# Key stacks of batch 0 sent first, later loads behind unit 0's queries, and a new order of jobs

## The reference, cut to what matters

```python
# layer 0 attention; layer 1 has the same form, with a mask over the context rows
q = (jnp.einsum('bld,ed->ble', x, Wq) + bq).reshape(b, l, h, dh)
kv = (jnp.einsum('bmc,ec->bme', y, Wkv) + bkv).reshape(b, m, h, 2 * dh)
k, v = (kv[..., :dh], kv[..., dh:])
att = jax.nn.softmax(jnp.einsum('blhd,bmhd->blmh', q, k) * scale, axis=2)
out = jnp.einsum('blmh,bmhd->blhd', att, v).reshape(b, l, d)

x = x + _L0_xattn_ref(_layernorm(x, axis=-1), ctx_768, ...)
x = x + _L0_ffn_ref(_layernorm(x, axis=-1), ...)
x = x + _L1_xattn_ref(_layernorm(x, axis=-1), ctx_768, mask_BxS2_bf1, ...)
x = x + _L1_ffn_ref(_layernorm(x, axis=-1), ...)
```

## Time and profile before

| | us |
|---|---|
| median of 3 runs | 402.03 (400.43 to 406.7) |
| the profiled execution | 399.99 |
| its span in the trace | 398.2 |
| TensorE busy | 306.9 (77%) |
| VectorE busy | 261.8 (66%) |
| ScalarE busy | 157.7 (40%) |
| GpSimd busy | 95.6 (24%) |

### The profile page before, as it was taken

How to read it: one execution, slowest core, us unless ns; L and a number is a source line. 1 busy time by engine, 2 the same in 40 slices (tenths; PEclk the granted TensorE clock), 3 DMA queues, 4 the chain that set the end, 5 groups by cost and what they waited for, 6 DMA issues and landing times.

```text
span 398.2 us, 4774 instructions
## 1 busy us (share of the span) xinstructions
PE 306.9 (77%) x1454; PEld 183.6 (46%) x1455; DVE 261.8 (66%) x682; ACT 157.7 (40%) x253; POOL 95.6 (24%) x103
## 2 busy tenths in 40 slices
PE   3476797788888627215667898898998999999995
PEld 1253433435345312013334325253457868888884
DVE  4457545585728168875777426675358699988883
ACT  3010435245463228231224236464663455454542
POOL 3701181010101079311107000101100761421500
PEclk9999959699999757655556569999999999999999
DMA  8962120300000930301311202000000000000000
GB/s 183 197 176 59 45 45 7 81 2 7 2 7 2 226 74 0 106 2 45 87 27 38 49 1 65 23 5 6 3 0 2 2 0 26 2 16 11 2 27 26
DMA packets 11914, 16.77 MB, mean 42 GB/s; under 512 B 3480, under 2 KB 6632, under 8 KB 11881
## 3 DMA queue, kind: packets, MB, share of 16 engines
q1 hardware_dynamic: 10018, 11.75, 12.0%
q0 software_dynamic: 1472, 4.26, 4.6%
q10 hardware_dynamic: 400, 0.45, 0.6%
HBM read 4.74 MB, written 1.05 MB: 15 GB/s over the span
## 4 chain that ended last, share of the span: by engine, by line
PE 59%; DVE 26%; ACT 5%; issue 4%; POOL 3%; DMA 2%; SPq 0%; DVEq 0%; POOLq 0%; ACTq 0%
PE ps_acc L1092 11%; PE ps_tok L938 6%; PE ps_key L947 5%; DVE mx L642 5%; PE ps_acc L1062 4%; PE ps_acc L1064 4%; PE ps_acc L1063 4%; DVE xn L569 3%; DVE stats L559 3%; PE ps_m L980 2%; PE ps_tok L1049 2%; PE ps_tok L1051 2%; PE ps_tok L1050 2%; PE ps_m L957 2%; POOL kst L347 2%
## 5 line engine op out<-in xcount | busy, mean ns | idle before, releaser
L642 DVE TENSOR_REDUCE mx<-ps_tok 128x4 f32<-128x312 f32 x128 | 57.4, 475 | 36.1 <-PE ps_tok L938 35.2
L445 ACT ACTIVATE big<-ps_key 104x512 f32<-104x512 f32 x96 | 55.2, 595 | 55.5 <-PE ps_key L947 54.3
L938 PE MATMUL ps_tok<-kst,qst 97*128 97x312 f32 x128 | 58.1, 479 | 15.8 <-DVE mx L642 15.4
L336 POOL TENSOR_SCALAR veps<-mv 128x4 f32<-128x4 f32 x16 | 3.7, 230 | 228.3 <-DVE mv L562 228.3
L938 PEld LDWEIGHTS ps_tok<-kst,qst 97*128 97x128 f32 x128 | 30.5, 245 | 51.9 <-DVE mx L642 26.9
L947 PE MATMUL ps_key<-qst,kst 105*104 105x512 f32 x96 | 44.9, 480 | 3.9 <-ACT big L445 2.0
L784 DVE TENSOR_TENSOR qst<-big,qst 128x512 fp32r<-128x512 f32 x64 | 44.3, 692 | 2.2
L782 DVE CAST qst<-big 128x512 fp32r<-128x512 f32 x64 | 27.0, 422 | 9.7 <-ACT big L505 9.5
L505 ACT ACTIVATE big<-ps_tok,b 128x512 f32<-128x512 f32 x32 | 21.9, 689 | 25.1 <-PE ps_tok L1051 24.9
L1092 PE MATMUL ps_acc<-big,vbd 104*32 104x512 f32 x192 | 29.9, 699 | 0.7 <-ACT big L445 0.7
L505 ACT ACTIVATE big<-ps_key,b 128x512 f32<-128x512 f32 x32 | 22.0, 691 | 21.3 <-PE ps_key L1051 20.8
(11 more groups left out here) (193 smaller groups left out, 546.8 us busy)
## 6 DMA issues: line engine op xcount, KB each, us to landing
qst<-qhi SPq DMA_DIRECT2D x64, 64.0 KB, 2.0
qst<-qlo SPq DMA_DIRECT2D x32, 64.0 KB, 2.0
w1f<-in_w POOLq DMA_DIRECT2D x2, 1024.0 KB, 7.9
kst<-rbuf POOLq DMA_DIRECT2D x12, 156.0 KB, 6.1
kst<-rbuf SPq DMA_DIRECT2D x12, 156.0 KB, 7.5
x<-in_x SPq DMA_DIRECT2D x4, 256.0 KB, 8.3
out<-xn SPq DMA_DIRECT2D x4, 256.0 KB, 2.0
qst<-mthl SPq DMA_DIRECT2D x32, 16.0 KB
```

What stands on the lines that cost most here:

```text
L445: act.activation(p[:, j, :], key[n % 2][0:PR, :], ACT.Exp, scale=SCALE).then_inc(q["p_ready"], 1)
L642: nc.vector.tensor_reduce(mx[:, u % 2, t, g, 0, :], tok[n % 2][:, 0:KG].rearrange("p (j h) -> p h j", h=HG), AX.X, ALU.max).then_inc(q["to ...
L938: mm(tok[n % 2][:, 0:KG], qst[0:MASKROW + 1, s, g, 128 * t:128 * t + 128], kst[0:MASKROW + 1, b, g, :], start=True, stop=True).then_inc(q[ ...
```

## The change

- The widening is a function of a range of batches. `key_split(0)` widens batch 0 only and raises `k_first`; a new job `kwide`, behind `lnx0` 0 on VectorE, widens batches 1 to 3 and raises `k_split`.
- GpSimd issues twelve transfers for batch 0, computes `rstd` of batch 1, waits for `k_split`, issues twelve for batches 1 to 3, and computes `rstd` of batches 2 and 3. The second twelve have semaphores of their own (`kst_in[2]`), for which `tok` of units 1 to 3 and `key_split(1)` wait.
- SP issues the mask, FFN weights, `bo` and `clip` behind unit 0's twelve query moves and ahead of unit 1's.
- The numbers of the order are new. What they change on the engines: in layer 0 TensorE does `vr0` twice before unit 0's `q`, the first `tok` before unit 1's `xt`, `q` of the next unit behind `tok` 7 instead of `tok` 2 (unit 1 to 3), `key` 0 behind four `tok` of the next unit instead of two, `ot` a `tok` later; VectorE does `on` 0 before `round` 1. In layer 1 TensorE does `xt` of the unit after next before `max` (for `max` 0 and 1), and `key` comes closer together; VectorE does `hround` 3 behind `tok` 5 instead of `tok` 14, and `lnx` 3 behind unit 5's `tok` 7 instead of `tok` 4.

```diff
         AT = (
             dict(
-            xt=[-32.1],
-            q=[-29.6],
-            tok=[-15.5 + 0.75 * c for c in range(NT * G)],
-            max=[-4],
-            pv=[7.1, 8.1, 11.4, 12.1, 15.1, 16.1],
+                xt=[-32.091],
+                q=[-26.662],
+                tok=[-16.267 + 0.753 * c for c in range(NT * G)],
+                max=[-4],
+                pv=[7.1, 8.1, 11.4, 14.206, 15.1, 16.1],
...
             dict(
-            xt=[-32.3],
-            q=[-29.3],
-            max=[-3.9],
-            key=[2 + 0.85 * j for j in range(NC * G)],
+                xt=[-35.965],
+                q=[-29.652],
+                max=[-3.203],
+                key=[1.987 + 0.733 * j for j in range(NC * G)],
...
-        BESIDE = dict(vr0=[-28.6, -25, -12.2, -10.4], lnstat=[-34.5, -26, -12, 4], lnx0=[-34, -23, -8, 8],
-                      nt=[29.8, 46.3, 62.3, 78.3], round=[12, 20, 28], wqt=[46, 48, 51, 53], kt=[55], vr=[56.1, 58, 60.8, 62.1])
+        BESIDE = dict(
+            kwide=[-30.2],
+            vr0=[-27.461, -27.296, -11.925, -9.845],
+            lnstat=[-35.568, -23.099, -13.806, 4.078],
+            lnx0=[-30.348, -21.819, -9.915, 7.66],
+            round=[14.104, 19.969, 30.533],
...
-        FFN = dict(hround=[-42, -41, -15, -5], down=[-40.1, -31.7, -13.1, -3.1], lnx=[-37.6, -25, -9, 4],
-                   gset=[30], x1=[31.1, 48.6], experts=[64.5 + 0.914 * n for n in range(NH)])
+        FFN = dict(
+            hround=[-50.361, -41, -15.005, -11.191],
+            down=[-37.329, -31.874, -12.818, -0.755],
+            lnx=[-35.088, -27.34, -9.108, 5.898],
+            experts=[64.5 + 0.952 * n for n in range(NH)],
...
@@ SP
+            def late_loads():
+                sp.dma_start(cmask[:, :, 0:M], a["mask"].partition_broadcast(128)).then_inc(q["mask_in"], 16)
...
+                        if u == 0:
+                            late_loads()
@@ GpSimd
-            pool.wait_ge(q["k_split"], 1)
-            for g in range(G):
-                for r, half in enumerate((0, 0, 1)):
-                    pool.dma_start(kst[32 * r:32 * r + 32, :, g, :].bitcast(F32),
...
-            for b in range(1, B):
+            pool.wait_ge(q["k_first"], 1)
+            key_stack(0, 1, kst_in[0])
+            rstd_of(1)
+            pool.wait_ge(q["k_split"], 1)
+            key_stack(1, B, kst_in[2])
+            for b in range(2, B):
                 rstd_of(b)
@@ VectorE, key_split
-                for half, src in enumerate((khi, klo)):
-                    for hh_ in range(HG):
-                        ins = nc.vector.tensor_scalar(kbd[:, half, :, hh_], src[:, :].bitcast(F32), kmask[:, hh_:hh_ + 1], None, ALU.mult)
-                ins.then_inc(q["k_split"], 1)
+                if L == 0:
+                    keys_widened(0, 1).then_inc(q["k_first"], 1)
+                else:
+                    keys_widened(0, B).then_inc(q["k_split"], 1)
...
+                    if job == "kwide":
+                        keys_widened(1, B).then_inc(q["k_split"], 1)
@@ TensorE, tok
+                            if L == 0 and b > 0:
+                                pe.wait_ge(kst_in[2][g], 48)
```

More of the change, by code:

```diff
@@ L198, in build @@
         stack_q = [[sem(f"stack_q{i}_{g}") for g in range(G)] for i in range(2)]
-        kst_in = [[sem(f"kst_in{i}_{g}") for g in range(G)] for i in range(2)]
+        kst_in = [[sem(f"kst_in{i}_{g}") for g in range(G)] for i in range(3)]
         stack_m = [[sem(f"stack_m{i}_{g}") for g in range(G)] for i in range(2)]
@@ L235, in build @@
-        BESIDE = dict(vr0=[-28.6, -25, -12.2, -10.4], lnstat=[-34.5, -26, -12, 4], lnx0=[-34, -23, -8, 8],
-                      nt=[29.8, 46.3, 62.3, 78.3], round=[12, 20, 28], wqt=[46, 48, 51, 53], kt=[55], vr=[56.1, 58, 60.8, 62.1])
-        FFN = dict(hround=[-42, -41, -15, -5], down=[-40.1, -31.7, -13.1, -3.1], lnx=[-37.6, -25, -9, 4],
-                   gset=[30], x1=[31.1, 48.6], experts=[64.5 + 0.914 * n for n in range(NH)])
+        AT = (
+            dict(
+                xt=[-32.091],
+                q=[-26.662],
+                tok=[-16.267 + 0.753 * c for c in range(NT * G)],
+                max=[-4],
+                key=[2 + 1 * j for j in range(NC * G)],
+                pv=[7.1, 8.1, 11.4, 14.206, 15.1, 16.1],
+                copy=[16.595],
+                on=[19.082],
+                ot=[21.311],
+                wo=[23.746],
+                ln=[26.718],
+            ),
+            dict(
+                xt=[-35.965],
+                q=[-29.652],
+                tok=[-15.5 + 0.75 * c for c in range(NT * G)],
+                max=[-3.203],
+                key=[1.987 + 0.733 * j for j in range(NC * G)],
+                pv=[6.352, 9.141, 11.1, 11.9, 14.244, 16.391],
+                copy=[17.2],
+                on=[19.768],
+                ot=[22.384],
+                wo=[23.775],
+                ln=[25.942],
+            ),
+        )
@@ L245, in build @@
         AT_YT, AT_Y, AT_LOG, AT_A, AT_B, AT_C = HLAG + 2, HLAG + 3, 12, 13, 15, 5
         FIRST_LOG, FIRST_A, FIRST_B, FIRST_C = 5, 6, 8, 12
-        ACT_LATE = dict(copy=0.4, key=0.2)
-        DVE_LATE = dict(on=0.1)
+        ACT_LATE = dict(copy=0.467, key=0.01)
+        DVE_LATE = dict(on=0.145)
         def order(L, late={}):
@@ L270, in _ @@
             sp.dma_start(kextra[96:97, :], a["krow"]).then_inc(q["mask_in"], 16)
[L271 to L278, removed]
+            def late_loads():
+                sp.dma_start(cmask[:, :, 0:M], a["mask"].partition_broadcast(128)).then_inc(q["mask_in"], 16)
+                for w, src in ((wg0, a["w_gate"]), (wu0, a["w_up"])):
+                    sp.dma_start(w[:, 0:2, :], src[0:256, :].rearrange("(t p) d -> p t d", p=128)).then_inc(q["wffn_in"], 16)
+                    sp.dma_start(w[0:IT[2], 2, :], src[256:I0, :]).then_inc(q["wffn_in"], 16)
+                sp.dma_start(wd0[:, :], a["w_down"]).then_inc(q["wffn_in"], 16)
+                sp.dma_start(bo[:, :], a["bo"].partition_broadcast(128)).then_inc(q["bo_in"], 16)
+                sp.dma_start(clip[:, :], a["clip"].partition_broadcast(128)).then_inc(q["clip_in"], 16)
             def move(dst, src, done):
@@ L343, in _, with key_stack @@
                 done(nc.gpsimd.memset(ap, value), "const_set")
-            pool.wait_ge(q["k_split"], 1)
-            for g in range(G):
-                for r, half in enumerate((0, 0, 1)):
-                    pool.dma_start(kst[32 * r:32 * r + 32, :, g, :].bitcast(F32),
-                                   kbd[32 * g:32 * g + 32, half, :, :].rearrange("p (b j) h -> p b (j h)", b=B).bitcast(F32)
-                                   ).then_inc(kst_in[0][g], 16)
-            for b in range(1, B):
+            def key_stack(b0, b1, landed):
+                for g in range(G):
+                    for r, half in enumerate((0, 0, 1)):
+                        pool.dma_start(kst[32 * r:32 * r + 32, b0:b1, g, :].bitcast(F32),
+                                       kbd[32 * g:32 * g + 32, half, b0 * MP:b1 * MP, :].rearrange("p (b j) h -> p b (j h)", b=b1 - b0).bitcast(F32)
+                                       ).then_inc(landed[g], 16)
+            pool.wait_ge(q["k_first"], 1)
+            key_stack(0, 1, kst_in[0])
+            rstd_of(1)
+            pool.wait_ge(q["k_split"], 1)
+            key_stack(1, B, kst_in[2])
+            for b in range(2, B):
                 rstd_of(b)
```

31 lines of the change are left out of this document (14 added, 17 removed).

## The result

The changed kernel takes 380.36 us (380.0 to 382.0). The kernel before, on the same chip beside it, took 401.23 us (400.27 to 406.7). The ratio is 0.9495, with an interval from 0.9451 to 0.954: five per cent faster, where the prediction had 393.9 us and a range down to 386. The ratio leaves out executions more than 1.5% above the fastest of the same kernel, here the one at 406.7 us. The profiled execution took 380.41 us with a span of 378.3; before it was 399.99 and 398.2.

A forecast was written before the change was run, and what follows sets the result against it. Before 300 us neither TensorE nor VectorE was taken as full: the order of jobs decides, with TensorE's clock often low. Terms -1.3 - 0.4 - 2.0 - 6.5 + 2.1 = -8.1 took the median from 402.03 to 393.9 us, range 386 to 405.

The forecast's parts named there:

- The head (-1.3): Start to the copy of `max` 0: split widening and stacks bring `xt` 1 sooner, -1.3 us, bounds -2.0 and +2.9.
- Unit 1 (-0.4): Unit 1's scores: `key` 0 behind four `tok` no longer waits 0.37 us for the moves, -0.4 us.
- Unit 2 (-2.0): Unit 2's scores: `on` 0 before `round` 1 removes most of 2.47 us idle before `ot` 0; bounds 0 and 5.
- my lower bound: Unit 2's scores: gain of 0, if the next maximum is late instead.
- a higher clock in unit 2 too: Rival: unit 2 gains three us more and unit 5 comes nearer to unit 7; 386 to 390 us, chance 0.12.
- Unit 5 (-6.5): Unit 5's scores, layer 1: later `lnx` 3 makes it as short as unit 6, -6.5 us, bounds 1.9 and 8.9.
- The rival in which only 1.4 us are won: Unit 5 stays at the low clock and gives 1.4 to 2 us; 398 to 401 us, chance 0.27.
- under 2.2 us: Sign that the forecast holds: `lnx` 3 of layer 1 takes under 2.2 us, with no 3.6 us gap.
- `xt` ahead of `max` (+2.1): `max` 0 and 1 of layer 1: transposes wait for the `xt` copy, 1.05 us each, +2.1, bounds 0 and 2.6.
- The rival "slower": Two TensorE waits within 5 us at `max` 1 of layer 1 lower unit 6's clock; about 410 us, chance 0.08.
- my signs of being wrong: The clock still falls in unit 5, or two `max` copies of layer 1 stay over 22 us apart.

The follow-up runs named there:

- s_only: Changed kernel with the old order of jobs, keeping only the split widening, split key stacks and later loads: 401.64 us, ratio 1.0007.
- q7: Kernel before with the next unit's `q` behind `tok` 6 instead of `tok` 2 in layer 0, unit 0's order kept: 392.31 us, ratio 0.9716.
- fill1: Kernel before with eleven useless matmuls added on TensorE at unit 1's two waits (0.80 and 1.15 us), nothing moved: 395.81 us, ratio 0.9768.
- round_late: Kernel before with only `round` 1 moved behind `on` 0 on VectorE: 400.66 us, ratio 0.994.
- w2_early: Kernel before with GpSimd's split of w2 two batches earlier, between `rstd` of batches 1 and 2 of layer 1: 404.68 us, ratio 0.9989.
- fill5: Kernel before with 22 useless matmuls added on TensorE before unit 5's `tok` 7, at the 3.61 us wait, nothing moved: 395.30 us, ratio 0.9865.
- xt_back: Changed kernel with `xt` of layer 1 behind `max` again (units 4 and 5): 379.66 us, ratio 0.9437.
- l0_new: Changed kernel with the order numbers of layer 1 and the experts as before: 385.86 us, ratio 0.9561.

## Why the prediction was wrong, step by step

**The head (-1.3): right.** Predicted and measured: twelve issues 6.6 and 6.94 us; first query issued at 15.4 and 14.99; `xt` 1 at 20.3 and 20.62; SP free at 31 and 29.39; `max` 0 at 35.6 and 35.48; its moves at 38.3 and 38.18. The later loads cost nothing. But `s_only` finds nothing of this 1.3 in the total, though its interval is no narrower than that: in its profile a start one microsecond sooner was swallowed by units 1 and 2.

**Unit 1 (-0.4): the step that failed.** "Unit 1's `q` is now behind `tok` 7" stands in the prediction, and was costed on SP's queue alone. What it does on the two engines that work there was not looked at: `qlo` leaves the middle of the maxima there, and the two waits of TensorE for them go, and with them the fall of the clock. It measured -6.1 us in the profiles. `q7` finds 3.7 of it with this number alone, and `fill1` finds 3.85 by filling the two waits and moving nothing.

**Unit 2 (-2.0): right place, wrong mechanism, and size too small.** I took most of the 2.47 us of idle time, and had the clock only in the bound. It measured -4.33. `round_late` makes the one move that I had costed, and wins 0.2 us in unit 2, because the next maximum comes late instead; that was my lower bound. The unit is this short only in profiles whose clock stays at 1.00 through it, and that needs the clock of unit 1. The rival "a higher clock in unit 2 too" was right in its mechanism, but it had no price for unit 1, and so 386 as its lower end.

**Unit 5 (-6.5): the number right, in part by luck.** The blocked `lnx` 3, the wait and the clock behind it are the reasons given, but the size was borrowed from unit 6 and not worked out. Measured -6.60, of which `xt` ahead of `max` took 1.04 back, so 7.6 against 6.5. The rival in which only 1.4 us are won falls. The Trainium skill, "SBUF — State Buffer", under "Who interferes with whom", has it that of VectorE and GpSimd the one that comes second to their shared port pair fully blocks. The trace agrees: VectorE's four instructions end 0.86 us after GpSimd's split in the changed kernel, 0.85 before, 0.58 in `w2_early`. More than half of what is won lies in the clock of the 15 us behind the wait, as `fill5` shows: in it VectorE is blocked as long as ever, and unit 5 is 3.7 us shorter. The rest is the shorter wait. My "under 2.2 us" for `lnx` 3 was 2.44: it began with 1.58 us of the split left, not 0.9.

**`xt` ahead of `max` (+2.1): right**, 1.04 and 1.11 by `xt_back`. The rival "slower" rested on this: two waits within 5 us bringing the clock down as the 3.61 us did. The two waits came, 0.99 and 1.14 us, and the clock stayed at 1.00 in the windows from 212 to 222. The sum for that rival was wrong besides: 409.3 takes for unit 6 the 18.8 us of unit 7, where unit 6 had 21.1, and leaves out the -6.5 of unit 5. With both put right, 6.5 us more in unit 6 would have made about 400.

None of my signs of being wrong came: the clock didn't fall in unit 5, and no two `max` copies of layer 1 stayed over 22 us apart. None of them was about unit 1, where half of the miss was.

**The rest.** Unit 7 became 0.6 us longer, which I had put at nothing; `xt_back`, with 19.38 us there too, shows that `xt` isn't its cause, and no run tells which of the other numbers of layer 1 is. The stage from `max` 3 to `max` 4 is 2.3 us shorter. The kernels with the same order there, `l0_new` and `xt_back`, have only about 1 us of it in their profiled executions, so half of it lies between executions of one order, and the cause of the other half stays open.

The fault behind all of this is one: I treated the clock as a matter of unit 5, where a wait of 3.6 us stood out, and not as a price on every group of waits. The earlier trace rows showed the same low digits at 50 and 70 us. A window or two over those slices would have shown the waits of 0.80 and 1.15 us, their engine, and the job of VectorE that lies among them.

## What to carry to other kernels

Where the slices show a low granted clock behind a stretch of waits, price the waits by the busy time behind them at half speed, not by their own length alone: here 1.95 us of waiting in unit 1 cost 5.3 besides themselves (`fill1`: 3.85 in unit 1, 1.44 in unit 2, in the fastest of its four executions). When a job is moved, ask on every engine that it touches what stood behind it, the short stall of another engine above all. To find out whether the clock or the idle time is the cause, fill the gap with useless matmuls and move nothing; a kernel that gets faster by doing more has answered. It answers for the clock's part only, since the filler keeps the gap: `fill5` leaves 2.9 us of unit 5's gain to the wait itself. And look for where a wait went before you say that it is gone: in `round_late` it stood one `tok` further on.

## What the runs showed of the hardware

- The clock isn't governed by the length of a single wait. It stayed at 1.00 over waits of 0.84 us (at 50.6) and 1.02 us (at 63.0) in the changed kernel, over 0.99 and 1.14 within 5 us, and fell behind 0.80 and 1.15 within 2 us in the kernel before. Once low, it stayed low over 14 us in which TensorE was busy 2.00 of every 2.00 us (222 to 236). What decides isn't settled by these runs.
- Extra work can pay: with eleven matmuls more the kernel was 2.3% faster (0.9693 to 0.9843), with twenty-two 1.3% (0.9786 to 0.9943).
- The granted clock reads 1.00 from the start of a trace to its first change, whatever the matmuls do: 0.63 us for one of 312 columns at 35.73 us, 0.41 at 46.40.
- An issue of a transfer on GpSimd's queue cost 0.55 to 0.58 us, whatever it carried: twelve of 39 KB took 6.94 us, twelve of 117 KB 6.58, twelve of 156 KB 6.64. Cutting these transfers in two doubled their price on the issuing engine, from 6.64 to 13.52 us.
- While GpSimd's split ran, VectorE's maxima from PSUM kept their 0.49 us each; its four instructions from SBUF to SBUF took up to 7.09 us together, instead of 1.11.
